# Two heads' outputs packed into 32 rows ahead of the output projection

## The reference

```
scores = einsum('bqhd,bkhd->bhqk', q, k) / sqrt(16)
attn   = softmax(scores, axis=-1)
out    = einsum('bhqk,bkhd->bqhd', attn, v).reshape(B, Lq, 256)
return x_q + (out @ Wp + bp)
```

## Time and profile before

| what | value |
|---|---|
| time, median of 3 runs | 437.83 us (436.24 to 439.31) |
| the profiled execution | 438.28 us, of which its span is 436.4 us |
| mean granted clock of PE | 0.995 |
| busy: PE, DVE, ACT, POOL | 420.4, 296.2, 223.5, 184.4 us |
| PE's busy time from 100 to 350 us | 49.58, 49.87, 48.76, 49.64 and 48.71 of each 50 us |

### The profile page before, as it was taken

How to read it: one execution, slowest core, us unless ns; L and a number is a source line. 1 busy time by engine, 2 the same in 40 slices (tenths; PEclk the granted TensorE clock), 3 DMA queues, 4 the chain that set the end, 5 groups by cost and what they waited for, 6 DMA issues and landing times.

```text
span 436.4 us, 9624 instructions
## 1 busy us (share of the span) xinstructions
PE 420.4 (96%) x3613; PEld 382.9 (88%) x3613; DVE 296.2 (68%) x748; ACT 223.5 (51%) x487; POOL 184.4 (42%) x192
## 2 busy tenths in 40 slices
PE   7989999999999999999999899999999899979996
PEld 6578999989998899989998799889988898868875
DVE  2785566774766696749863896499548865891787
ACT  2868644255347633763367236734672356326271
POOL 6445473553543445324623453256334732341020
PEclk9999999999999999999999999999999999998999
DMA  8777101631100221024000300030003021300301
GB/s 293 241 290 283 50 2 43 164 85 31 44 5 2 63 60 29 26 61 134 2 5 13 110 2 5 9 89 2 5 15 84 0 49 34 80 4 26 72 3 49
DMA packets 16982, 27.94 MB, mean 64 GB/s; under 512 B 3816, under 2 KB 9256, under 8 KB 16808
## 3 DMA queue, kind: packets, MB, share of 16 engines
q1 hardware_dynamic: 16808, 27.32, 21.5%
q10 hardware_dynamic: 128, 0.01, 0.0%
HBM read 16.07 MB, written 2.10 MB: 42 GB/s over the span
## 4 chain that ended last, share of the span: by engine, by line
PE 76%; DVE 15%; issue 3%; ACT 3%; DMA 1%; SPq 1%; ACTq 0%
PE hidden_banks L1709 7%; PE hidden_banks L1710 7%; PE hidden_banks L1711 7%; PE score_banks L1716 6%; PE score_banks L2081 5%; PE token_bank L1709 5%; PE token_bank L1710 5%; PE token_bank L1711 5%; PE score_banks L2051 4%; PE value_bank L2104 3%; DVE head_maxima L1473 3%; PE value_bank L2107 3%; PE value_bank L1716 3%; PE hidden_banks L1934 2%; DVE sums L1487 2%
## 5 line engine op out<-in xcount | busy, mean ns | idle before, releaser
L1632 POOL TENSOR_TENSOR hidden_low<-hidden,hidden_high 128x512 fp32r<-128x512 f32 x56 | 72.7, 1298 | 117.1 <-ACT hidden_high L1078 117.0
L1709 PE MATMUL hidden_banks<-normed_high,hidden_w_high 128*128 128x256 f32 x224 | 64.2, 287 | 0.8 <-issue 0.8
L1473 DVE TENSOR_REDUCE head_maxima<-score_banks 128x2 f32<-128x308 f32 x128 | 54.4, 472 | 14.3 <-PE score_banks L2051 12.2
L1710 PE MATMUL hidden_banks<-normed_high,hidden_w_low 128*128 128x256 f32 x224 | 62.5, 279 | 0.0
L1711 PE MATMUL hidden_banks<-normed_low,hidden_w_high 128*128 128x256 f32 x224 | 62.4, 279 | 0.0
L1140 ACT ACTIVATE exp_ring<-score_banks 128x512 f32<-128x512 f32 x96 | 52.6, 600 | 18.8 <-PE score_banks L2081 17.9
L1078 ACT CAST hidden_high<-hidden 128x512 fp32r<-128x512 f32 x56 | 34.8, 621 | 48.3 <-DVE hidden L1390 46.6
L1709 PE MATMUL token_bank<-expert_out_high,hidden_high 128*128 128x256 f32 x192 | 55.6, 290 | 0.0
L1070 ACT ACTIVATE hidden<-hidden_banks 128x512 f32<-128x512 f32 x56 | 33.3, 596 | 40.7 <-PE hidden_banks L1934 39.0
L1711 PE MATMUL token_bank<-expert_out_low,hidden_high 128*128 128x256 f32 x192 | 53.4, 278 | 0.0
L1710 PE MATMUL token_bank<-expert_out_high,hidden_low 128*128 128x256 f32 x192 | 53.4, 278 | 0.0
(11 more groups left out here) (289 smaller groups left out, 1112.5 us busy)
## 6 DMA issues: line engine op xcount, KB each, us to landing
unit_weights<-units SPq DMA_DIRECT2D x7, 768.0 KB, 6.0
query_stack<-queries_high SPq DMA_DIRECT2D x56, 64.0 KB, 2.0
tokens<-x SPq DMA_DIRECT2D x8, 256.0 KB, 3.6
query_stack<-queries_low SPq DMA_DIRECT2D x28, 64.0 KB, 2.0
w_slice<-units SPq DMA_DIRECT2D x7, 256.0 KB, 3.1
out<-tokens SPq DMA_DIRECT2D x7, 256.0 KB, 2.4
w_T<-folds SPq DMA_DIRECT2D x6, 256.0 KB, 6.2
pair_keys<-keys_high SPq DMA_DIRECT2D x16, 77.0 KB
```

Source lines behind the costliest of these rows:

```text
L1473: v.tensor_reduce(MX[:, s, first:first + step + 1:step], S[:, ring_of[key][0], 0:2 * CTX].rearrange("p (j n) -> p j n", j=2), AX.X, ALU.ma ...
L1632: nc.gpsimd.tensor_tensor(SL[:, ring(t, u), :], TB[:, ring(t, u), :], raw(SH[:, ring(t, u), :]), ALU.subtract).then_inc(gpsimd_h, 1)
L1709: mm(out_, lh, rh, start=start, stop=False, skip_group_check=skip)
L1710: mm(out_, ll, rh, start=False, stop=False, skip_group_check=skip)
```

## The change

The outputs of two groups are packed into the 32 rows, so that four groups become two packs. For groups with an odd number the outputs lie in the lower 16 rows and the sums above them; for even groups it is as before. The output stage has 512 columns instead of 1024, and the projection has 12 matmuls for a tile (2 packs by 2 halves of the tokens by 3) instead of 16.

- `dup` is now two DVE instructions of 128x512 with a wait between them: multiply the even group by a mask column (`own_rows`), then add the odd group times the other mask (`other_rows`).
- POOL's `sum` is one step after half 1, four instructions: an add of 128x512, two multiplies of 128x256 by a mask column, an add of 128x256, with a wait after the first and one after the third. Its order in POOL's list is that of the second step before. For `LAST` the sums are made on DVE in the step `sums`, by two more instructions each.
- `out` has two shuffles instead of four, and `outl` is a plain subtraction of 128x512; ACT's cast is 128x512.
- In the setup `proj_w` is half as large, its low part is one POOL instruction of 128x512 instead of two of 128x1024 (L1666, L1669), and `key` on DVE writes the values (L1331) in two instructions and their tail (L1336) in four instead of two.
- ACT's `raw` waits for `dup` and `sum` of the tile before, no longer for `out`.

```diff
             def sums(key):
                 t, h = key[1:]
                 total = sums_of(t, h)
-                dve.wait_ge(gpsimd_sum, upto(gpsimd_sum, ("sum", t, 1 if t < LAST else h), "s"))
+                if t == LAST:
+                    dve.wait_ge(scalar_raw, upto(scalar_raw, ("raw", t, h), "v"))
+                    v.tensor_scalar(total[:, :], RAWL[:, 2 * h, :], other_rows, None, ALU.mult).then_inc(vector_results, results.one())
+                    dve.wait_ge(vector_results, results.n)
+                    v.scalar_tensor_tensor(out=total[:, :], in0=RAWL[:, 2 * h + 1, :], scalar=own_rows, in1=total[:, :],
+                                           op0=ALU.mult, op1=ALU.add).then_inc(vector_results, results.one())
+                    dve.wait_ge(vector_results, results.n)
+                else:
+                    dve.wait_ge(gpsimd_sum, upto(gpsimd_sum, ("sum", t), "s"))
                 v.reciprocal(total[:, :], total[:, :]).then_inc(vector_sums, 1)
...
-                v.stream_shuffle(out_tiles(t)[3][:, g, :], raw_of(t)[:, g, :], [i % DH for i in range(32)]).then_inc(vector_dup, 1)
+                v.tensor_scalar(packed, both[:, :, 0, :], own_rows, None, ALU.mult).then_inc(vector_results, results.one())
+                dve.wait_ge(vector_results, results.n)
+                v.scalar_tensor_tensor(out=packed, in0=both[:, :, 1, :], scalar=other_rows, in1=packed,
+                                       op0=ALU.mult, op1=ALU.add).then_inc(vector_dup, 1)
...
-                v.scalar_tensor_tensor(out=both[:, g, :], in0=raw(high[:, g, :]), scalar=CN[:, C_HEAD + 1:C_HEAD + 2], in1=twice[:, g, :],
-                                       op0=ALU.mult, op1=ALU.subtract).then_inc(vector_outl, 1)
+                split_low(low_[:, g, :], packed[:, g, :], high[:, g, :]).then_inc(vector_outl, 1)
...
             def sums(key):
-                t, h = key[1:]
-                pool.wait_ge(scalar_raw, upto(scalar_raw, ("raw", t, h), "v"))
-                if h == 0:
-                    if 0 < t < LAST:
-                        pool.wait_ge(vector_out, upto(vector_out, ("out", t - 1, 0), "o"))
-                    nc.gpsimd.tensor_tensor(sums_of(t, 0)[:, :], raw_of(t)[:, 0, :], raw_of(t)[:, 1, :], ALU.add).then_inc(gpsimd_sum, 1)
-                elif t == LAST:
-                    nc.gpsimd.tensor_tensor(SUML[:, :], RAWL[:, 2, :], RAWL[:, 3, :], ALU.add).then_inc(gpsimd_sum, 1)
-                else:
-                    pool.wait_ge(gpsimd_sum, upto(gpsimd_sum, ("sum", t, 0), "s"))
-                    nc.gpsimd.tensor_tensor(SUM[:, :], SUM[:, :], RAW[:, 2, :], ALU.add).then_inc(gpsimd_part, 1)
-                    pool.wait_ge(gpsimd_part, t + 1)
-                    nc.gpsimd.tensor_tensor(SUM[:, :], SUM[:, :], RAW[:, 3, :], ALU.add).then_inc(gpsimd_sum, 1)
+                t = key[1]
+                pool.wait_ge(scalar_raw, upto(scalar_raw, ("raw", t, 1), "v"))
+                if t:
+                    pool.wait_ge(vector_out, upto(vector_out, ("out", t - 1, 0), "o"))
+                if t == NEXT:
+                    pool.wait_ge(tensor_z, upto(tensor_z, ("z", LAST, NU - 1), "z"))
+                both = out_tiles(t)[0]
+                nc.gpsimd.tensor_tensor(both[:, :, :], RAW[:, 0:2, :], RAW[:, 2:4, :], ALU.add).then_inc(gpsimd_part, 1)
+                pool.wait_ge(gpsimd_part, 3 * t + 1)
+                nc.gpsimd.tensor_scalar(both[:, 0, :], both[:, 0, :], other_rows, None, ALU.mult).then_inc(gpsimd_part, 1)
+                nc.gpsimd.tensor_scalar(both[:, 1, :], both[:, 1, :], own_rows, None, ALU.mult).then_inc(gpsimd_part, 1)
+                pool.wait_ge(gpsimd_part, 3 * t + 3)
+                nc.gpsimd.tensor_tensor(SUM[:, :], both[:, 0, :], both[:, 1, :], ALU.add).then_inc(gpsimd_sum, 1)
...
-            def proj_part(t, s, groups):
-                both = out_tiles(t)[2]
+            def proj_part(t, s, packs):
+                _, high, low_, _ = out_tiles(t)
                 c = slice(P * s, P * s + P)
-                for g in groups:
-                    mm(proj_bank(t, s), both[:, g, c], WPh[:, g, :], start=(g == 0), stop=False)
-                    last = mm(proj_bank(t, s), both[:, g, c], WPl[:, g, :], start=False, stop=(g == GROUPS - 1))
+                for p in packs:
+                    last = exact(proj_bank(t, s), (high[:, p, c], low_[:, p, c]), (WPh[:, p, :], WPl[:, p, :]), p == 0, p == PACKS - 1)
                 return last
```

More of the change, by code:

```diff
@@ L284 @@
     "score": (32, 32.1, 32.1, 32.7, 33.5, 33.7, 34.2, 34.3, 34.3, 35.4, 35.5, 35.6),
-    "value": (33.88, 34.18, 35.92, 36.25), "raw": (35.5, 36.9), "sum": (35.3, 36.4), "sums": (38.1, 47.7),
+    "value": (33.88, 34.18, 35.92, 36.25), "raw": (35.5, 36.9), "sum": 36.4, "sums": (38.1, 47.7),
     "out": (38.34, 56.69), "outl": (43.37, 97.85), "bias": 26.2, "proj": 43.6, "last": (16, 59.3), "reload": 45.3, "init": 5.2,
@@ L402, in schedule @@
         for h in range(2):
-            for name in ("raw", "sum"):
-                place(at + plan(t, name)[h], (name, t, h))
+            place(at + plan(t, "raw")[h], ("raw", t, h))
+        if t < LAST:
+            place(at + plan(t, "sum"), ("sum", t))
         for h in range(parts_of(t)):
@@ L438 @@
     "score": lambda t, w: SCORES * t + w, "value": lambda t, g: GROUPS * t + g,
-    "raw": lambda t, h: 2 * t + h, "sum": lambda t, h: 2 * t + h,
+    "raw": lambda t, h: 2 * t + h,
 }
@@ L511, in build @@
         WQl = put("query_w_low", [P, KC, D], F32R)
[L512 to L513 removed]
+        WPh = put("proj_w_high", [P, PACKS, D], F32R)
+        WPl = put("proj_w_low", [P, PACKS, D], F32R)
         A = put("score_w", [P, BATCH, KC, CTX + EXPERTS])
@@ L633, in build @@
         assert after <= exps_at
-        WPR = put("proj_w_raw", [P, GROUPS, D], offset=exps_at)
+        WPR = put("proj_w_raw", [P, PACKS, D], offset=exps_at)
         at[0] = max(end1, end2)
@@ L1148, in raws @@
                 elif t:
-                    act.wait_ge(vector_out, upto(vector_out, ("out", t - 1, 0), "o"))
+                    act.wait_ge(vector_dup, upto(vector_dup, ("dup", t - 1, 0), "d"))
+                    act.wait_ge(gpsimd_sum, upto(gpsimd_sum, ("sum", t - 1), "s"))
                 nc.scalar.copy(raw_of(t)[:, 2 * h:2 * h + 2, :], halves(V0[:, :])).then_inc(scalar_raw, 1)
@@ L1491, in dup @@
                 t, h = key[1:]
-                g = groups_of(t, h)
+                g = packs_of(t, h)
+                packed = out_tiles(t)[3][:, g, :]
+                both = raw_of(t)[:, :, :].rearrange("p (q o) n -> p q o n", o=2)[:, g]
                 dve.wait_ge(scalar_raw, upto(scalar_raw, ("raw", t, 1 if t < LAST else h), "v"))
@@ L1559, in setup_values @@
                     for g in range(GROUPS):
-                        p.memset(VA[b][:, 4 * g:4 * g + 4, DH + 4 * g:DH + 4 * g + 4], 1.0)
-                        last = p.tensor_copy(VT[b][:, 4 * g:4 * g + 4, DH + 4 * g:DH + 4 * g + 4],
+                        columns = slice(sum_row(g), sum_row(g) + 4)
+                        p.memset(VA[b][:, 4 * g:4 * g + 4, columns], 1.0)
+                        last = p.tensor_copy(VT[b][:, 4 * g:4 * g + 4, columns],
                                              CN[:, C_ROW:C_ROW + 4].unsqueeze(2).to_broadcast([P, 4, 4]))
@@ L2127, in proj @@
                 for s in range(NSUB):
-                    last = proj_part(t, s, range(GROUPS))
+                    last = proj_part(t, s, range(PACKS))
                 last.then_inc(tensor_proj, 1)
@@ L2134, in lead @@
                 for s in range(NSUB):
-                    proj_part(t, s, range(GROUPS // 2))
+                    proj_part(t, s, range(1))
             def last_proj(key):
```

83 lines of the change are left out of this document (40 added, 43 removed).

## The result

The changed kernel takes 442.89 us (median of 4 runs, 440.93 to 444.02) against 437.15 us for the kernel before beside it (436.24 to 439.31): a ratio of 1.0122, 95% interval 1.0098 to 1.0146. It is 1.0 to 1.2% slower; the prediction said 443.0.

What follows compares the result with a forecast made beforehand. PE, busy 96%, was taken to bound the kernel, stalled by POOL's longer sum. Terms 3.6-0.25+0.55+0.45+0.9 gave +5.2 us: 443.5 on the profiled 438.28, hence 443.0 as median, range 435.5 to 448.

Steps and rivals of the forecast that it cites:

- POOL's step: POOL's sum after half 1: four instructions take 3.82 us against 1.52, so `prob`, deviation and low part come 2.30 later.
- S: Start of POOL's first add after the copy of half 1; 151.18 us in tile 0 before the change.
- Contention: c: how long DVE's packing pair holds POOL back; 0 to 1.0 us, taken as 0.6.
- PE's stall: PE's products of the low part, tiles 0, 2, 3: 1.35 us later plus c of 0.6; +1.2 net each.
- The products: Four projection products fewer a tile on PE: 0.46 us each for tiles 0 to 4, -2.3 us.
- Tiles 1, 4, 5: Net effects of the change in these tiles: -0.25, +0.55 and +0.45 us.
- The end: Tiles 6 and 7: later reciprocal and DVE's extra sums against shorter output steps, +0.9 us.
- The setup: POOL loses 3.9 us of work, DVE gets 0.65 more twice, under PE work that waits for neither: 0.
- Cheap multiplies (1): POOL's mask multiplies cost 0.20 us each like the 16-column copy: -2.6 us, 435.2; chance 0.14.
- full lockouts with dearer multiplies (3): DVE and POOL block each other in full and POOL's multiplies cost more: 446 to 450 us; chance 0.15.
- POOL's step binding nobody (2): POOL's longer sum delays neither DVE's reciprocal nor PE, only savings stand: -5.7 us, 432.1; chance 0.06.
- Rival 4: Half of PE's stall is won back by DVE's lighter load later in the tile: 438 to 440 us; chance 0.11.

Runs made afterwards that it cites:

- d3_no_packing: Changed kernel with DVE's two packing instructions replaced by one shuffle of the even groups, odd groups left out: 440.87 us, ratio 1.0084.
- e3_sums_on_dve_shift: Changed kernel with the sum split between POOL (early) and DVE, code shifted by 32 small products ahead, two warm-up products out: 450.03 us, ratio 1.0311.
- c1_again: Changed kernel, untouched, measured a second time: 442.02 us, ratio 1.0104.
- d2: Changed kernel with POOL's sum cut to two adds (masks, one group left out) and 16 projection products a tile instead of 12: 434.20 us, ratio 0.9932.
- e2: Changed kernel with POOL's sum cut to two adds, 12 products, code shifted by 32 small products ahead, two warm-up products out: 444.48 us, ratio 1.0202.
- e1_code_shift: Changed kernel, whole, with 32 small products put ahead of everything on PE and two of four warm-up products out: 454.71 us, ratio 1.0417.
- d4: Changed kernel without the two masking instructions ahead of each DVE reciprocal in tile 7; one group's sums taken straight from the copy: 439.92 us, ratio 1.0050.
- c2_short_sum: Changed kernel with POOL's sum cut to two adds of 128x256, masks and one group's sums left out: 433.81 us, ratio 0.9908.
- c3_sum_later: Changed kernel with POOL's sum of tiles 0 to 5 behind the low part, DVE's reciprocal and spreading later too: 459.10 us, ratio 1.0483.
- d1_sums_on_dve: Changed kernel, whole, sum split: POOL masks and adds groups 0 and 1 after half 0, DVE adds groups 2 and 3: 437.49 us, ratio 1.0002.

## Why the prediction was right, and where it was not

The sign, the cause and the place came out as forecast. That 443.0 lies within 1 us of 442.89 and 442.02 is partly luck: the mechanism's own terms come to +2.7 us where +5.2 was said, and two things that the prediction didn't have, the transfers and the clock, make up most of the rest.

**POOL's step** carried the sign and most of the size. Predicted S+3.82 without contention, measured S+4.01 (d3_no_packing) and S+4.06 with it: the multiplies cost 0.93 alone, not 0.86 (I had taken the fixed part of one from a copy, 0.20; 0.93 for 256 columns and 2.86 for 1024 make it 0.29). The copy of 16 columns and L1643 as ends held, and L1669 was the row to take. The Trainium skill ("GPSIMD Engine Reference", section "Engine selection") has such operations near line rate; 0.93 us for 256 columns is 3.6 ns a column, and the trace disagrees.

**Contention** was mis-sized: c = 0.6 us on POOL, 0.05 measured by d3_no_packing. I had the two engines share the delay; here DVE, which came second, bore nearly all of it (1.08 us for 0.47) and POOL ran on. The rows that I cited could have told: in the trace of before L1336 of DVE (1.09 us) started 0.29 behind a POOL instruction of 1.29, and L1643 of POOL (2.20) 0.50 behind a DVE instruction of 1.60. In both the second one pays, and DVE's pair starts second. The Trainium skill ("SBUF — State Buffer", section "Who interferes with whom") has the port held for a whole instruction; DVE's 0.61 us fits that, and so does the small multiply of e3_sums_on_dve_shift, which ends 0.03 us after the POOL instruction it started behind.

**PE's stall** in tiles 0, 2 and 3 was put at 1.95 us and is 1.66 (S+7.14 against S+5.48). The errors above, +0.19 and -0.55, explain that but for 0.07. The wait on maxima that it absorbs was put at 0.3 and is 0.40: in c1_again PE is behind the kernel before by 0.97 us ahead of tile 0's output, 2.61 behind the stall, 2.21 one unit later, 1.72 after the four products. That is +0.75 a tile where +1.2 was said; tile 3 gives +0.72.

**The products**: 0.46 a tile predicted, 0.45 in c1_again in each of tiles 0 to 4, 0.46 by d2 and e2.

**Tiles 1, 4, 5:** tile 1 was +0.2 and -0.46, and comes out at -0.45. Tile 4 was put at +0.55, measured +0.27 with 0.08 of it the transfer's wait. Tile 5 was put at +0.45, and PE is 0.63 later there behind a wait for maxima (0.87 us, L1485), after the late reciprocal; 0.23 of it come back at the next wait, for a DMA of the maxima, so +0.40 is left (e1_code_shift takes 41.75 us from this second copy to the next, the kernel before 41.33, both with one stretch of half clock in it).

**The end** was put at +0.9: PE's wait ahead of the last projection goes from 1.27 to 2.54 us, and from tile 6's second copy to the end of the span c1_again loses 0.42. The masks' 0.95 a half was right (d4: 1.81 for both in the trace); more came back elsewhere than I counted.

**What was missing** is the transfer's wait: +0.64 us net in c1_again (1.95 for the changed kernel's three, 1.31 for the one of before). It lay in the trace of before, 1.61 us at tile 2, but no step of the change touched it, except that the number of instructions a tile did. My sum of +5.2 is +2.7 by these pieces (0.75-0.45+0.63+0.72+0.19+0.40+0.42), +3.3 with the transfers; the measured difference is 4.3 to 5.7 us.

**The setup and the clock** hold the remainder. I had put the setup at 0. In c1_again it is 0.96 longer: 0.69 because PE's clock came up at 7.33 us and not at 5.83 (4.28 to 6.77 in seven other profiles of the same setup, so this part is chance), and 0.26 in front of a product that waits for DVE behind the divided instructions of `key` (0.39 us from the start before it, at 88.65; 0.13 in the kernel before, at 87.67). All eight profiles with the changed setup and the code in its place have 0.38 to 0.55 there, so that 0.26 belongs to the change. Of the ten executions of the changed kernel three had the clock at full throughout, 440.05, 440.93 and 441.11 us; of the eleven of the kernel before beside c1_again five had, with a median of 437.02. Between these medians lie 3.9 us, and the pieces above with the transfers and the 0.26 give 3.6. What the medians of all executions show on top goes with stretches of the clock at half. One place of them is on the path: in the first profile and in e1_code_shift the last twelve products start 0.21 us apart and not 0.12, which costs 1.09 us (11.31 us from the last copy to the end, 10.22 in c1_again). Ahead of these products PE has the wait that the change makes longer, 2.54 us. In c1_again and c3_sum_later the clock held through the same wait; in no profile with a shorter one did it fall there. That the longer wait makes such a fall more likely is thus suggested by four profiles, not shown.

**The rivals.** Cheap multiplies (1) is out, by 0.93 us, and full lockouts with dearer multiplies (3) by the 0.05. POOL's step binding nobody (2) is what c2_short_sum shows with the step gone: 433.8 against my 432.1 for it. Rival 4, half the stall won back, describes the trace partly (0.40 of 1.64 us), but not its time.

## What to carry to other kernels

Price a step by what is queued behind it on its engine. POOL is busy 43% of the time, and 2.5 us more on it, put between a copy and what two other engines wait for, cost 8 us, more than all the products saved; half of the same work ahead of the copy, where POOL idles, with the rest on DVE, gave 4.5 back. But moving work also moves what stands behind it: there a multiply of 0.17 us came to start behind a POOL instruction and took 1.21. When the number of instructions in a loop changes, look where the code's own packets fall: a gain of 0.46 us a tile was eaten by transfers that nobody had touched, and one kernel against another can differ by 3 us in 436 for this alone, so a product's price is better read between two points of the trace than from the whole time.

## What the runs showed of the hardware

**Code packets delay a queue's issues.** A transfer's issue of 0.59 us takes 0.8 to 2.0 when a 16 KB packet of instructions starts with it (61 of 63 long issues).

**The clock falls after a pause of PE.** In c3_sum_later each pause of 1.9 to 2.8 us at a maxima product in tiles 0 to 3 was followed 0.8 to 1.2 us after its end by the granted clock at half. The windows view of tile 0 (columns: length, busy time and count of PE, its weight loads, DVE, ACT, POOL, then the clock):

```profile
164.40:165.30 0.90, 0.90 (x7) 0.90 (x8) 0.87 (x3) 0.00 (x0) 0.00 (x0) 0.97 0.00 0
165.30:168.70 3.40, 3.40 (x18) 3.40 (x17) 2.60 (x6) 1.14 (x2) 0.87 (x1) 0.50 0.00 0
168.70:172.10 3.40, 3.40 (x27) 3.20 (x27) 1.46 (x3) 0.00 (x0) 3.23 (x3) 1.00 0.03 5
```

18 products at 1.2 GHz in the time of 27 at 2.4 GHz. So each of these four pauses cost itself and some 1.7 us on top; the stalls of 0.7 us in the changed kernel had no such effect. Such a pause doesn't always do it: in the same run PE pauses 2.7 us in tile 4 as well, until 358.1, and the clock stays. Ahead of tile 6's scores PE pauses 2.1 us at 393.4 in the kernel before and the clock falls at 394.9, and 2.35 us at 397.3 in c1_again, where it stays.

**DVE's multiply waits out a POOL instruction, however small it is.** DVE's multiply of 128x2 took 1.21 to 1.22 us for 0.17 in six places where it started 0.08 to 0.09 us behind a POOL instruction of 1.27 (tiles 0, 2 and 3 of d1_sums_on_dve and of e3_sums_on_dve_shift); DVE's shuffle of 128x512 took 0.75 beside POOL's add of 1.30 (d3_no_packing).

**Tiny products are not cheap, and didn't bring the clock up.** At the lower clock 64 instructions with 4 columns, each behind a 128x128 fp32 set of weights, took 13.65 us, 0.21 each. That is what an instruction of 256 columns took at half clock at the end of the first profile, with weights in fp32r. The clock stayed low through all 64, while in the kernel before it had come up by 5.8 us. No run has such products at the higher clock.
